# One fused two-layer kernel on one core: the hand-written orders of all five engines, and the table of its seven accumulator banks, written anew

## The reference, cut to what matters

```python
xn = _layernorm(x)
x = x + _L0_attn_ref(xn, ...) + _L0_ffn_ref(xn, ...)
xn = _layernorm(x)
x = x + _L1_attn_ref(xn, ...) + _L1_ffn_ref(xn, ...)

# attention, 16 heads of 8 values (layer 0 adds biases, an RMS norm of q and k, a sigmoid gate and Wo)
energy = jnp.einsum('nhqd,nhkd->nhqk', q, k)
attn = jax.nn.softmax(energy / jnp.sqrt(jnp.float32(hd)), axis=3)
out = jnp.einsum('nhql,nhld->nhqd', attn, v)

# experts: the two best of 16 (layer 0, plus a shared expert) or of 8 (layer 1) for each row
w, idx = jax.lax.top_k(jax.nn.softmax(logits), 2)
y = silu(x @ W_gate) * (x @ W_up) @ W_down        # of each chosen expert, weighted by w
```

## Time and profile before

| | us |
|---|---|
| median of 3 runs (607.15 to 614.67) | 612.5 |
| the profiled execution, its own time | 612.57 |
| span of its instructions | 610.7 |
| TensorE busy by the profile (95%) | 583.1 |
| VectorE busy (80%) | 488.6 |
| ScalarE busy (69%) | 420.5 |
| GpSimd busy (51%) | 310.1 |

### The profile page before, as it was taken

One profiled execution on the slowest core, in us unless ns is written; L12 is line 12 of the kernel. 1 busy time (PEld: TensorE's weight loads), 2 busy tenths in 40 slices (PEclk: granted clock), 3 DMA queues, 4 the chain that ended last, 5 costly groups with the idle time before them and its releaser, 6 DMA issues. The chain is left out here.

```text
span 610.7 us, 12039 instructions
## 1 busy us (share of the span) xinstructions
PE 583.1 (95%) x3727; PEld 317.0 (52%) x3727; DVE 488.6 (80%) x1075; ACT 420.5 (69%) x827; POOL 310.1 (51%) x428
## 2 busy tenths in 40 slices
PE   7868999989999999999999999999999999999996
PEld 5533343555654555543645765576556557555321
DVE  7999999897797899998767889777657839759942
ACT  3623766877788887977866765677766586765794
POOL 7058646277735646188772545475353723204550
PEclk9975999899999999999999999999999999999998
DMA  7274132365566564346734637636654773451210
GB/s 251 88 231 161 38 105 73 99 186 165 160 194 192 145 178 135 88 131 200 225 110 150 194 103 215 221 116 211 195 166 127 234 206 115 160 147 36 76 45 26
DMA packets 68382, 90.03 MB, mean 147 GB/s; under 512 B 8416, under 2 KB 55264, under 8 KB 67808
## 3 DMA queue, kind: packets, MB, share of 16 engines
q1 hardware_dynamic: 64224, 80.87, 42.8%
q0 software_dynamic: 4096, 8.40, 4.8%
HBM read 66.04 MB, written 22.81 MB: 145 GB/s over the span
## 5 line engine op out<-in xcount | busy, mean ns | idle before, releaser
L1068 DVE TENSOR_REDUCE mx<-slot 128x1 f32<-128x512 f32 x512 | 320.5, 682 | 71.5 <-PE slot L646 69.5
L812 ACT ACTIVATE probsT<-slot 128x512 f32<-128x512 f32 x512 | 273.1, 608 | 81.0 <-PE slot L661 79.3
L646 PE MATMUL slot<-k_stack,q_stack 72*128 72x512 bf16 x512 | 165.3, 392 | 6.5 <-DVE mx L1068 3.9
L661 PE MATMUL slot<-q_stack,k_stack 75*128 75x512 bf16 x512 | 161.4, 384 | 2.3 <-DVE mx L1068 0.8
L674 PE MATMUL pv_ps<-probsT,v 128*32 128x512 f32 x1024 | 124.1, 604 | 0.0
L1182 POOL TENSOR_TENSOR hid<-th,up 128x512 f32<-128x512 f32 (+2 forms) x56 | 70.9, 1272 | 90.3 <-DVE th L925 89.2
L646 PEld LDWEIGHTS slot<-k_stack,q_stack 72*128 72x128 bf16 x512 | 49.0, 99 | 85.1 <-issue 27.9
L661 PEld LDWEIGHTS slot<-q_stack,k_stack 75*128 75x128 bf16 x512 | 47.7, 98 | 76.8 <-issue 27.7
L1159 POOL DMA_INDIRECT xs_hbm<-xn,index x64 | 63.8, 997 | 29.7 <-issue 14.8
L1170 POOL DMA_INDIRECT yg<-ys_hbm,index x64 | 61.6, 963 | 22.3 <-issue 18.2
L623 PEld LDWEIGHTS slot<-xgT,wbuf 128*128 128x128 f32 (+1 forms) x552 | 66.1, 182 | 7.3 <-issue 1.2
(11 more groups left out here) (138 smaller groups left out, 559.3 us busy)
## 6 DMA issues: line engine op xcount, KB each, us to landing
wbuf<-in_experts SPq DMA_DIRECT2D x46, 544.0 KB, 4.9
q_stack<-parts_hbm SPq DMA_DIRECT2D x32, 288.0 KB
k_stack<-parts_hbm SPq DMA_DIRECT2D x96, 96.0 KB
wbuf<-in_experts SPq DMA_DIRECT2D x62, 128.0 KB, 2.2
parts_hbm<-parts SPq DMA_DIRECT2D x16, 384.0 KB, 3.7
xg<-xs_hbm SPq DMA_DIRECT2D x24, 256.0 KB, 3.0
ys_hbm<-ys SPq DMA_DIRECT2D x24, 256.0 KB, 4.4
xs_hbm<-probsT SPq DMA_DIRECT2D x2, 2048.0 KB, 9.2
```

Of the source, the lines that this page charges most:

```text
L646: nc.tensor.matmul(ps[:, 0:N], q_stack[0:STACK, h, j * P:(j + 1) * P], k_stack[0:STACK, h, :], start=True, stop=True).then_inc(slot_full, 1)
L661: nc.tensor.matmul(ps[:, 0:N], k_stack[0:STACK + MAXROWS, h, j * P:(j + 1) * P], q_stack[:, h, :], start=True, stop=True).then_inc(slot_fu ...
L812: nc.scalar.activation(probsT[:, k % PROBS, a, :], ps[:, 0:N], ACT.Exp, scale=SCALE).then_inc(slot_free, 1)
L1068: nc.vector.tensor_reduce(mx[:, g, u // J, u % J:u % J + 1], ps[:, 0:N], AXIS.X, ALU.max)\
```

## The change

The five texts of `ORDER` and the text `SLOT` are replaced. Each engine does the same stages as before, each kind in the same order among itself; only how the kinds are interleaved, and which of the seven slots a fill uses, differ. No other line changes. The first lines of each text, and one later line of TensorE's:

```diff
     "PE": """
-XT QV3 XT QV SG SU SG SU QK2 QV4 RK M5 XT M4 QK M8 QK XT M QV M3 NT QV M3 QV2 M SD M2 E2 M E2 M E M E2 M E M E
-M2 E7 NT M2 SD M3 PV2 M2 E M E QK E QK E M E M QV2 E M2 E M E2 M3 E M PV M3 NT QV E3 M2 E M E2 M6 PV E2 M E2
...
+XT QV4 SU SG XT SG QK2 QV4 RK M5 QK M2 SD XT M QK M2 SU M5 XT M6 NT QV M QV M3 SD M QV2 M E M E M2 E M E4 M2
+E3 PV E M NT M2 E2 M E M E M E M PV E2 M QK E3 QK M E M3 QV M2 E2 QV M E3 M3 PV M4 NT M E3 M2 E M2 QV M2 E PV
...
+RK M E2 PV GU E SG M E2 M PV M2 DN GU E SU AT E DN M E M OT M E M E OY E QK M XG M3 E M GU E M E2 DN PV NT M
...
+E2 M UU GG AT E PV E2 M E DN E M E PV E M2 E XG M E2 M E XT M2 E4 PV E M2 E2 M2 QK E GG UU M GG2 NT E PV QK AT
...
     "ACT": """
-XN XT XN XT SS SG SU SG QK HI QK HI MI2 SU RT SS XN XT QK HI XN QK GS HI XT NT E8 GS E6 NT E2 SS E2 QK E2 QK
...
+XN XT XN SU XT SS SG2 QK2 HI2 MI2 RT XN SS XT XN QK SU QK HI XT NT HI E GS E9 SS E NT E10 QK E QK E2 HI E3 NT
...
     "DVE": """
-LN2 QV SJ QV SJ QV SJ QV SJ HAND NM GA2 QV RE2 QV PT2 QV2 RT LN RW LN SS SL NM M19 SW M2 QV M4 QV2 M2 QV M7 SS
-M5 SD NM M SD M4 QV2 M9 QV M11 GS QV M4 RT AT M12 RW SS M2 GA M2 SL NM M2 GA2 AT M3 GA GS M3 HAND M3 HAND M OY
...
+LN2 QV SJ QV2 SJ QV SJ2 NM GA2 HAND QV RE2 QV2 PT QV RT PT RW LN SL SS LN NM M17 SW M QV M2 QV M3 SD M QV M3
+QV M5 SS M GS M5 NM SD M9 QV M4 QV M7 QV M7 QV M3 RT AT M12 RW GA M SL M SS M NM GA M3 GA AT GS HAND M4 OY GA
...
     "POOL": """
-LN3 SQ SC LN GA BO PT MP PT SC2 GA SQ MP SC BO SC4 MP2 PT2 SQ MP GA BO SC2 GA2 SC2 GA MP SC BO GA PT SC GA SC
...
+LN2 SQ LN GA SC2 BO LN SC2 GA MP BO SC PT2 SQ BO MP SC BO SC2 MP2 PT2 MP SQ GA SC2 GA3 SC MP SC4 GA2 SC MP GA3
...
     "SP": """
-ZERO PW RF4 ZERO WL3 NT WL3 PW NT RF WL2 NT XL NT XL WL RF XL PW NT WL XL WL RF WL5 RF YS WL2 XL2 WL YS WL NT
...
+ZERO PW RF2 WL2 ZERO NT WL2 RF WL2 PW WL NT RF WL2 RF XL WL XL WL NT WL2 RF NT WL3 XL WL2 XL NT WL3 RF PW XL
...
 SLOT = """
-01234560123450613450261345102630451263064531204153604162652415321634256143621543652413524051460352461305423651402536
...
+06152430615420361542036154204612463214061324046013624051413250154315240312405132450132541265023645213604561032651032
...
```

The very end of TensorE's text:

```diff
-PV E6 NT E PV E5 AT E3 PV E6 PV E11 PV2 AT
...
+E M E3 M E M E PV E M2 E M E M E5 PV NT E9 PV AT E9 PV E7 PV2 AT
```

More of the change, by code:

```diff
@@ L93 @@
[L93 to L97, removed]
@@ new lines @@
+E2 M E SU M3 QK M E XG M4 PV M E M E SG E M2 E2 XG GU E M3 DN SD M E M E GU E M PV M NT M E XG DN E XG E M3 GU
+E M2 GU M E2 SD XG M DN M2 E M E2 DN E4 M3 PV E2 M2 NT GU M2 DN E2 M2 E PV E M XG M E2 M E2 M GU M E M2 E AT
+E3 M2 PV NT E2 M3 E2 M E XG E2 PV M E M2 E M GU E2 M E2 M2 PV M2 E M E4 DN AT E4 M PV E NT M E M E OT M2 XG M3
+E2 DN GU M3 XT M2 PV M3 E QK OY E M XG M E3 M2 E DN M2 E QK E3 M GU E2 PV NT M2 E M E M DN E M XG VG E M5 PV M
+E2 XT AT M E QK E2 VG M E VG NT VG E M2 E3 M DN M2 E M2 E XG E M E2 GU E PV E RK E3 M E M GU M2 E PV E2 XG M
@@ new lines @@
+M2 E M2 GG E M UU M XG M E2 M2 E NT E DN M2 E2 M E M2 E M E PV E M E M E2 M2 E2 M E3 M2 PV M2 E2 M NT UU GG2
+UU GG UU E M2 E XG M3 E M DN E2 AT E3 PV M E2 M4 E4 PV M GG UU GG NT M UU GG M UU E M E2 M E M E M E DN E M2
+E2 M E PV M AT E XG M E2 M2 E2 M PV E2 M E M3 E M E M3 GG NT GG E UU GG E UU2 E2 PV E DN E M3 E M E M E2 M PV
+E2 M XG E M E M E M E PV M E NT E2 M E M2 E M GG M UU2 GG UU E2 GG M PV XG E2 M E M DN M E M2 E4 M3 AT E M E M
+E NT PV E M E2 M2 E M4 PV M4 UU GG2 UU E GG E M UU E NT M E M E2 XG E2 DN E M E4 M2 E PV E M2 E2 M PV E2 M3 E
@@ new lines @@
+E5 PO E7 GS NT HI E9 XG E2 RT E2 GU E3 XG E NT E7 XG E SS E GU SG E PO DN E SU E DN E OT GU E3 XG E QK E GU E2
+DN NT E3 QK E SU E2 XG E2 SG XG GU E DN E3 GU HI E NT E XG E2 XG DN E GU2 XG E DN E5 DN E2 HI E2 NT E PO E2 GU
+DN E XG E7 GU E3 NT E6 XG E5 GU E GS E PO E4 DN E6 NT E OT E XG E XN DN E XT GU QK E GS E XG E3 HI E2 DN QK E4
+NT E2 GU E2 XG DN E XN PO XT E3 HI E2 QK NT E6 DN E RT E XG E GU E7 GU E4 XG E2 QK NT E GU DN E9 DN E PO DN E
+NT E10 OT E2 HI NT E18 XG E PO E GG2 E UU E2 NT UU HI E GG E UU E4 XN E DN E3 XG E4 XT E6 GG QK UU GG E NT E
@@ new lines @@
+HI GG PO UU OT E UU E QK E2 DN E4 HI XN E4 XT E XG E NT E GG E GG UU E RT GG UU E UU E XG DN E5 QK E4 QK E2 NT
+E2 GG UU E GG E2 PO UU GG E UU XG E4 NT DN E14 UU NT GG2 E2 UU GG UU E4 XG E4 DN E5 PO E GG UU GG UU NT GG UU
+E3 HI E7 DN E4 XG E HI E5 GG E UU GG E NT UU GG UU E3 DN E8 PO E XG E2 NT E4 GG UU E UU GG UU E GG E XG E3 DN
+E10 NT E2 GG UU GG E UU GG E UU NT E4 XG E4 PO E8 DN E2 GG2 UU XG UU E2 GG UU E NT E3 DN E14 PO GG E UU GG UU
+E GG UU NT E5 XG DN E7 GG E UU E GG NT E2 GG UU E2 UU E5 PO DN E7 NT E16 NT E15 PO NT E25 PO
@@ L130 @@
-HAND AT M9 GA M GA M GA M13 AT M4 XA GA M GA2 M14 YC M GA M GA M4 GA M4 AT M5 HAND M10 GA M3 GA M GA M11 GA M
-GA M3 GA M2 YC M2 AT XA M12 GA3 M15 AT M2 GA2 M6 GA M7 HAND M8 AT M3 XA M22 YC2 AT2 XA
+LN2 QV SJ QV2 SJ QV SJ2 NM GA2 HAND QV RE2 QV2 PT QV RT PT RW LN SL SS LN NM M17 SW M QV M2 QV M3 SD M QV M3
+QV M5 SS M GS M5 NM SD M9 QV M4 QV M7 QV M7 QV M3 RT AT M12 RW GA M SL M SS M NM GA M3 GA AT GS HAND M4 OY GA
+M6 SW M GA M13 GA M3 GA M2 SD GA M9 GA SD M GA M11 GA M8 AT GA M4 HAND M8 GA M4 YC M AT LN GS M13 GA M OY M6
@@ L132 @@
+YC M2 LN M5 GA VG M5 AT M2 VG M VG2 M3 RT M4 RW M GA SL M3 GA M8 GA M HAND M19 GS M3 AT M8 SW M4 OY M9 GA M YC
+GA LN GA AT M13 YC GA2 HAND M2 AT M GA VG M OY M LN M7 VG M5 VG M VG M3 GA RT M GA M2 GA RW M12 SL M9 GA2 M6
+GA M4 SW M15 GA M GA2 M5 HAND M AT M6 GA M GA M GA M8 AT M10 GA M GA M GA M12 HAND XA M GA M3 GA M GA YC M8 AT
+M13 GA2 M GA HAND M4 YC M8 GA2 M4 GA M3 AT M4 XA M10 GA3 M17 GA M AT GA M6 GA M15 AT M23 XA YC AT YC AT XA
 """,
     "POOL": """
-LN3 SQ SC LN GA BO PT MP PT SC2 GA SQ MP SC BO SC4 MP2 PT2 SQ MP GA BO SC2 GA2 SC2 GA MP SC BO GA PT SC GA SC
@@ L146 @@
+YS XL NT RF WL2 XL2 WL NT RF WL2 YS XL PW NT WL RF WL4 NT XL RF YS WL RF WL3 NT PW WL RF YS NT WL3 XL WL YS NT
+RF WL2 XL RF WL NT WL4 YS2 XL NT RF XL WL3 NT YS RF WL RF WL3 NT XL2 WL PW YS NT WL2 RF WL2 YS RF NT WL4 XL NT
+RF WL RF YS OUT NT YS RF OUT YS NT3 OUT2
 """,
@@ L161 @@
+46305204632053426051432061320651342605132540623514063251406325104362510436250163524150631254063215406321450362145032
+46150243261563241563204516031245603124560321465031205463120546321302546130254613024156035240163520461532046153204615
+320461532046
 """
```

67 lines of the change are left out of this document (21 added, 46 removed).

## The result

| | runs | median us | range us | mean granted clock |
|---|---|---|---|---|
| before | 103 | 613.7 | 605.2 to 619.8 | 0.960 to 0.989 |
| after | 26 | 606.9 | 604.9 to 608.9 | 0.975 to 0.986 |

These pool all runs for which a clock is on record, but for one execution of before that took 1572 us. The first comparison, 20 runs of each, gave 606.91 us against 612.48, a ratio of 0.9939, 95% interval 0.9911 to 0.9967; the ratio leaves out runs over 1.5% above the fastest of their kernel, the medians count all. The forecast was 614.6 us: small as the change is, it went the other way.

What follows compares the result with a forecast made beforehand. The kernel was taken as a start bound by VectorE, a long middle bound by TensorE's own work and a short tail. The sum was 612.6 + 0 - 1.5 + 1.5 + 1 + 4 - 3 + 0 = 614.6 us, range 606 to 622.

Steps and rivals of the forecast that it cites:

- The rival: Slower by the clock: three half-clock stretches in TensorE's middle, 614.6 + 10 = 625 us; chance 0.05.
- Part 3: The middle, bound by TensorE: 13 `PV` close behind their last `E` cost 4 us, slots gain 3.
- The slots, -3: Middle: longer stretches between a slot's fill and its next use gain 3 us, bounds 0 and 8.
- Part 4: The tail, ScalarE's last 25 `E` and two `PV`: 0, with 1.5 us to either side.
- Part 1: Up to VectorE's first `M` at 41.16 us: same stages in another order, 0, with 1 us to either side.
- Part 2: VectorE-bound start, 41.2 to 141.8 us: existing waits shrink by 1.5 us, new waits cost 1.5 and 1.
- `SL` on `RK`: Start, second round: VectorE's `SL` waits 1.5 us for the mask behind TensorE's late `RK`, bounds 0 and 3.
- `NM` on the root: Start: VectorE's `NM` after the third `SS` waits for ScalarE's root and table load, 1 us, bounds 0 and 3.
- The two covers: Start: GpSimd's second `SQ` ends at 67.3 us with 1.8 to spare; SyncE's third `RF` issued by 59.5; both cost 0.
- GpSimd late for `SQ`: Slower rival: slower scatters and a later start put `SQ` 4 us beyond its cover, 619 us; chance 0.08.
- ScalarE late for the `PV`: Slower rival in the middle: 13 close `PV` wait 1.25 us each, 16 us instead of 4, 627 us; chance 0.12.
- The faster rival: VectorE's 6.7 us of start waits and half of the middle's 17 go, new waits cost 2.5: 600 us; chance 0.15.

Runs made afterwards that it cites:

- Experiment 1: The kernel before, unchanged, run twelve times for the clock of each run: median 607.8 us; its profiled execution took 606.3 us.
- Experiment 4: The new order with 23 more matmuls on zeros between 222 and 225 us: median 605.75 us, 604.7 to 607.65.
- Experiment 2: The old order with 13 more matmuls on zeros between 101 and 104 us: median 607.1 us, 605.5 to 608.8.
- Experiment 6: Zeros added in the start: new order with 23 and 58 zeros 606.25 us, with 14 more 603.8; old order with 13 and 87 zeros 605.05.
- Experiment 3: The new order, but every `PV` waits for all eight of its `E` before its first matmul: median 614.8 us, 7.9 more than the new kernel.
- its control: The old order with every `PV` waiting for all eight `E`: seven runs at 607.5 to 610.1 us, five at 615.5 to 618.4.
- the best version: The new order with 23 zeros at 222 us, 58 between 37 and 67 us and 14 at 69 and 70 us: 603.8 us.

## Why the prediction was wrong

The profiled executions differ by 5.5 us of span, 610.7 against 605.2, where the sum had +2. Experiments 1 and 4 split that with their spans. Before in its better execution takes 604.5 (-6.2: 1.1 ahead of 96 us, 4.4 up to the `NT` of the 96th `M`, 1.6 at the end, less the 0.8 that the middle gives back). After without its loss at 227 us takes 602.9 (-1.6 for the order), and 605.2 with it (+2.3, about half of it at 227 us, and half by which the two executions already differ at 139 us). These are single executions: the fastest runs of the two kernels without zeros are 605.2 and 604.9 us, so that the 1.6 may as well be nothing.

**The base of the sum** failed first. "The sum is made against the profiled execution, 612.57 us": that execution had 6.8 us at half clock, which I saw and priced at 3.4, but only as a rival for the new order, with 0.05. I took the old stretch for a fixed part of the kernel. It was an event of most of its runs, worth 4.4 us with what VectorE lost, and in the new order it is absent: from 80 to 112 us TensorE is busy for 31.54 of 32 us there, at 1.00. The rival had the right mechanism on the wrong kernel. The rule that I weighed there, of the Trainium skill, "TensorE: Matmul & The Clock Gate", section "A second HAM failure mode: psum-queue depth-cycling", holds that short idle spells between groups of matmuls make the clock swing. Experiments 2, 4 and 6 agree: zeros in such spells keep the clock at 1.00. Experiment 1 limits it: the same spells, once with and once without a loss. "The clock at 1.00 throughout" was wrong too, by the loss at 227 us.

**Part 3, the term of +4 for 13 close `PV`**, failed on a wait that I misread. "A `PV` cannot start before its last `E` has gone through the array and ScalarE": it can, and the description of `PV` ahead of it, "needs its eight `E` emptied", holds only for its end. The loop waits for the four `E` of one j, does 8 of the 16 matmuls, and only then waits for the other four. The timeline of after, all engines, around a `PV` right behind its `E`, where I counted the most:

```profile
325.41 0.38 PE L662 MATMUL slot<-q_stack,k_stack 75*128 75x512 bf16 x1
...
325.71 0.16 PEld L675 LDWEIGHTS pv_ps<-probsT,v 128*32 128x32 f32 x8 [0.27 <-issue]
...
325.82 0.60 ACT L813 ACTIVATE probsT<-slot 128x512 f32<-128x512 f32 x1
...
326.53 0.20 PEld L675 LDWEIGHTS pv_ps<-probsT,v 128*32 128x32 f32 x8 [0.66 <-ACT probsT L813]
```

The first eight weight loads start at 325.71, before ScalarE has even begun with the last `E` (325.82 to 326.42), and the other eight follow at 326.53. The half `PV` between is 0.93 us (1.85 / 2), and hides nearly all of the wait. Experiment 3 takes that cover away, and 6.8 us of waits come and 7.9 of time (some 2 of them in its control as well), beside the 9.0 of the upper bound. The pair of the earlier trace rows, 1.44 us, showed a distance in the text and not a need.

**The slots, -3.** In the executions of experiments 1 and 4, without those losses, the two orders stand at 136.63 and 138.16 us at the `NT` of the 96th `M`, and end at spans of 604.5 and 602.9: middle and tail together gain 3.1 us. Parts 3 and 4 said 4 - 3 + 0 = +1; with the `PV` at 0 they would have said -3. That slots are the mechanism is not shown: the waits at lines 637 and 662 are 1.9 and 1.1 us, no fewer than before.

**Part 1, 0:** the first `M` came at 42.22 us instead of 41.16, just outside the bound of 1. The sum has no term for instructions of VectorE that grow. In the new order GpSimd does its first `SQ` earlier, beside the routing; before, then after:

```profile
29.94 0.29 DVE L1011 TENSOR_TENSOR probs<-probs,prob_sum 128x128 f32<-128x128 f32 x1
31.16 1.89 POOL L1144 TENSOR_TENSOR rest<-qk_tok 128x1024 f32<-128x1024 f32 x1
```

```profile
27.76 1.89 POOL L1145 TENSOR_TENSOR rest<-qk_tok 128x1024 f32<-128x1024 f32 x1 [13.11 <-DVE parts L901]
28.05 1.75 DVE L1012 TENSOR_TENSOR probs<-probs,prob_sum 128x128 f32<-128x128 f32 x1
```

The instruction takes 1.75 us instead of 0.29 and ends 0.15 us behind GpSimd's; a second one (`place_ab`, 0.65 instead of 0.16) ends with GpSimd's next, at 36.8 us. That is 1.95 us, more than the delay. It is what line 1086 did in experiment 1. Both are read from traces; no run tested them.

**Part 2:** VectorE is idle for 8.2 us from 22.3 to 139.1 (116.8 less 19.19 + 26.00 + 7.18 + 31.66 + 24.58), where 7.7 - 1.5 + 1.5 + 1 = 8.7 was forecast, but by other terms; and its busy time, which the sum took as fixed, was 108.6 us instead of 111.8 (line 1086 of before makes 1.8 of the 3.2). `SL` on `RK` cost 0, not 1.5: the last matmul of `RK` ended 1.15 us behind the mask (113.15 to 114.30), not 2.3 as in the earlier trace rows, and that fits under the `GA` and the `M` that stand between; 0 was the lower bound. `NM` on the root cost 0.3, not 1. The waits that I let shrink did not: 3.9 us on `M` fills, and 2.8 of them is one wait at 70.8 us, where a `PV` at half clock took 3.64 us on TensorE and no `M` could pass it. That is a stall of the clock in the part that hangs on VectorE, which I had left out as harmless there; with the clock up the waits on `M` fills do shrink, to 1.4 us in the trace of experiment 1 and 1.2 in that of the best version. The two covers held: the second `SQ` ended at 68.12, against a forecast 67.3, and VectorE came at 68.04, so that the cover of 1.8 us is used up to nothing; the third `RF` was issued at 59.53 us, as forecast.

**Part 4, 0:** 25 exponentials in 12.36 us. The end of before lost 1.6 us to half clock, which the base carried as well.

**The other rivals.** GpSimd late for `SQ`: no, by a hair. ScalarE late for the `PV`: 16 us were priced, 0.2 came. The faster rival, 600 us, was right in its sign alone: VectorE's waits did not go.

## What to carry to other kernels

Before a sum is made against one execution, look whether its clock column has a stretch that other executions of the same kernel lack: here one such stretch cost 4.4 us, as much as the largest term that the change was given. A mean clock alone does not price such a loss: see where it falls, and what it pushes beside what. Read a wait inside a loop at the place where it stands, and count the work that may run ahead of it. Where TensorE pauses in short pieces and its clock falls behind them, try matmuls on zeros in the pauses: 13 of them in the old order did for the median what the new texts did, and 95 in the new order took another 3.1 us.

## What the runs showed of the hardware

- The same program with the same pauses (1.71 and 1.58 us busy of 2.00 each) loses its clock for 6.8 us in one execution and not in another. 67 of 103 runs of before lie in the group with the lower mean clock. What decides between the two is open.
- In three places TensorE did a `PV` (from 98.9, 220.8 and 66.1 us), then paused in pieces of 0.2 to 1.2 us, and then fell from the upper level (2.4 GHz) to the lower (1.2 GHz), for 6.8, 3.4 and 6.7 us.
- Holding the clock at one place can move the loss on: with zeros up to 67 us it was 1.00 until 71 us and fell there; with the next 14 zeros the profiled execution kept 1.00 there too.
- In four traces a short VectorE instruction that fell beside a computation of GpSimd ended within 0.2 us of it: 3.16 us instead of 0.19 (line 1086 of before, with half clock; 3.17 in two further traces), and 1.75 instead of 0.29 (after, 28.05 us).
